# Attention phase of a fused recurrent and feed-forward kernel: one small DMA sent by ACT instead of SP, low parts taken a third of a head later, and turned rows' banks by turns

## The reference, cut to what matters

```python
def _attention(x, Wq, Wk, Wv, Wo):          # 8 batches, 16 heads of 32 features
    q = (x @ Wq.T).reshape(b, s, H, HD)
    k = (x @ Wk.T).reshape(b, s, H, HD)
    v = (x @ Wv.T).reshape(b, s, H, HD)
    scores = jnp.einsum('bqhd,bkhd->bhqk', q, k) / np.sqrt(HD).astype(np.float32)
    scores = jnp.where(causal, scores, jnp.finfo(scores.dtype).min)
    probs = jax.nn.softmax(scores, axis=-1)
    out = jnp.einsum('bhqk,bkhd->bqhd', probs, v).reshape(b, s, d)
    return out @ Wo.T
...
mod = MOD_SCALE * jnp.tanh(attn @ A)
gate_pre = h @ W_in_base.T + mod * (h @ A) @ B
```

## Time and profile before

| | us |
|---|---|
| median of three runs | 2830.97 |
| profiled execution, its own time | 2831.37 |
| its span, first to last instruction | 2829.6 |
| attention in that span | about 870 to 1722 |
| PE busy over the span | 2561.5 |
| DVE busy | 1428.4 |
| ACT busy | 1073.6 |
| POOL busy | 380.9 |

### The profile page before, as it was taken

How to read it: one execution, slowest core, us unless ns; L and a number is a source line. 1 busy time by engine, 2 the same in 40 slices (tenths; PEclk the granted TensorE clock), 3 DMA queues, 4 the chain that set the end, 5 groups by cost and what they waited for, 6 DMA issues and landing times.

```text
span 2829.6 us, 38755 instructions
## 1 busy us (share of the span) xinstructions
PE 2561.5 (91%) x14359; PEld 2059.7 (73%) x14359; DVE 1428.4 (50%) x2943; ACT 1073.6 (38%) x1770; POOL 380.9 (13%) x353
## 2 busy tenths in 40 slices
PE   5899999999995688988898887999999999999997
PEld 4677778777774466766666766888888878888886
DVE  5666656656654356766676775221211423333333
ACT  4444444444442156655665674111111211111111
POOL 0000000000001223332334231000000001111111
PEclk8999999999996888988999987999999999999999
DMA  3000000000002344333433323111111322222212
GB/s 128 15 16 16 30 30 1 30 31 16 1 16 94 110 112 116 80 102 109 117 84 98 98 82 114 45 45 45 45 45 45 123 101 93 109 96 90 90 60 75
DMA packets 97728, 194.60 MB, mean 69 GB/s; under 512 B 22128, under 2 KB 22640, under 8 KB 91376
## 3 DMA queue, kind: packets, MB, share of 16 engines
q1 hardware_dynamic: 97536, 192.04, 21.6%
HBM read 99.43 MB, written 41.94 MB: 50 GB/s over the span
## 4 chain that ended last, share of the span: by engine, by line
PE 78%; DVE 9%; issue 5%; ACT 4%; POOL 2%; DMA 1%; SPq 1%; DVEq 0%; POOLq 0%; ACTq 0%
PE PS L72 13%; PE PS L74 13%; PE PS L73 13%; PE PS L1833 4%; PE PS L1834 4%; PE PS L1835 4%; PE PS L1432 3%; PE PS L695 2%; PE PS L693 2%; PE PS L1451 2%; PE PS L694 2%; PE PS L1408 2%; PE PS L1410 2%; PE PS L1409 2%; DVE PS L1621 1%
## 5 line engine op out<-in xcount | busy, mean ns | idle before, releaser
L1882 DVE TENSOR_TENSOR GF<-SG,PS 128x512 f32<-128x512 f32 x128 | 88.0, 687 | 619.4 <-PE PS L74 619.4
L1621 DVE CUSTOM_DVE_ANT_0 PS<-PS,MK 128x512 f32<-128x512 f32 (+3 forms) x512 | 243.7, 508 | 102.6 <-PE PS L1432 101.5
L1536 ACT ACTIVATE PF<-PS 128x512 f32<-128x512 f32 (+1 forms) x384 | 198.8, 524 | 161.1 <-PE PS L1453 152.6
L1856 ACT ACTIVATE SG<-PS 128x512 f32<-128x512 f32 x128 | 76.3, 596 | 429.6 <-PE PS L1815 429.6
L1451 PE MATMUL PS<-QS,KS 97*128 97x512 f32 (+3 forms) x512 | 184.3, 390 | 56.5 <-issue 42.8
L1432 PE MATMUL PS<-KS,QS 96*128 96x512 f32 (+3 forms) x512 | 183.5, 401 | 38.4 <-DVE MX L1621 38.1
L72 PE MATMUL PS<-XH,WH 128*128 128x512 f32 x512 | 212.1, 414 | 6.5 <-DVE XC L967 6.5
L1860 ACT CAST GH<-GF 128x512 fp32r<-128x512 f32 x128 | 79.3, 620 | 364.1 <-DVE GF L1882 364.1
L1913 POOL TENSOR_SCALAR XN<-XT,MEAN,RSTD 128x512 f32<-128x512 f32 x32 | 67.1, 2101 | 1041.9 <-DMA M<-m_scratch 726.2
L72 PE MATMUL PS<-FH,GW 128*128 128x512 f32 x512 | 200.3, 391 | 7.7 <-DVE DW L1877 7.7
L1833 PE MATMUL PS<-DW,GH 128*128 128x512 f32 x512 | 200.3, 391 | 5.4 <-DVE GL L1884 5.4
(11 more groups left out here) (277 smaller groups left out, 5930.5 us busy)
## 6 DMA issues: line engine op xcount, KB each, us to landing
QS<-QT SPq DMA_DIRECT2D x384, 64.0 KB, 2.0
KS<-QT SPq DMA_DIRECT2D x384, 64.0 KB, 2.0
FH<-rh_scratch SPq DMA_DIRECT2D x16, 1024.0 KB, 5.6
FL<-rl_scratch SPq DMA_DIRECT2D x16, 1024.0 KB, 8.0
XF<-in_x_dram SPq DMA_DIRECT2D x32, 256.0 KB, 3.5
s_scratch<-ZS SPq DMA_DIRECT2D x8, 1024.0 KB, 4.3
STGB<-in_x_dram SPq DMA_DIRECT2D x8, 1024.0 KB, 6.7
rh_scratch<-RH SPq DMA_DIRECT2D x8, 1024.0 KB, 8.7
```

What stands on the lines that cost most here:

```text
L1536: act.activation(PE_[u][:, o:o + at], PS[4 + a % 2][:, 0:at], ACT.Exp, scale=SC).then_inc(a_ex, 1)
L1621: dve.tensor_tensor_reduce(out=p[:, at:at + n], in0=p[:, at:at + n], in1=MK[:, 512 - n:512], scale=1.0, scalar=NEG, op0=ALU.add, op1=ALU.m ...
```

## The change

One table by third of a head takes the place of the generator `attn_order`, and several kinds of steps get a second name, one or a few thirds later, at which the engine that needs another engine's result takes its turn. PE's steps keep their thirds.

- ACT sends the DMA from NM to QS (`largest_out`), one third after it has negated the maxima. SP no longer has a step `largest_in`.
- One third later than before stand on DVE the low parts of turned rows (`normal_low`) and of queries and keys (`project_low`), on ACT, DVE and POOL the splitting of the values (`values_split`), on ACT the copy of the low-rank product (`low_rank_out`), on POOL its piece of the remainder (`remainder_end`). ACT still copies turned rows, queries and keys in the third in which PE computes them.
- DVE's four operations after every fourth head stand at thirds 17, 19, 20 and 21 instead of all at 17; the modulation's at one, two and three thirds after the transposition instead of in the same third.
- The four turned rows of a batch use banks 0, 1, 0, 1 instead of 0, 1, 1, 0.
- The second `largest_in` of a batch and the `modulation` each share a third with a piece of `project`; they now stand ahead of it.

The core of the diff:

```diff
-        for kind, bank, at in (("normal", (0, 1, 1, 0), (46, 47, 0, 1)), ("values", (1, 1, 1, 1), (14, 16, 25, 27)),
-                               ("largest_in", (0, 1, 1, 0), (42, 6, 18, 30)), ("low_rank", (1,), (38,)),
-                               ("modulation", (0,), (10,))):
...
+        for third in range(-72, 3 * HEADS + 24):
+            g, p = divmod(third, 3)
...
+            if p == 0 and 0 <= g - 1 < HEADS:
+                at(third, "remainder", g - 1)
+            if p == 1 and 0 <= g - 1 < HEADS:
+                at(third, "remainder_end", g - 1)
...
+        for b in range(NB):
+            t = 48 * b - 48
...
+            for d, third, bank in ((0, -2, 0), (1, -1, 1), (2, 0, 0), (3, 1, 1)):
+                bank_of["normal", b, d] = bank
+                at(t + third, "normal", b, d)
+                at(t + third + 1, "normal_low", b, d)
+            for r, q, k in ((0, 3, 8), (1, 14, 20), (2, 25, 31), (3, 36, 42)):
+                for n, third in ((0, q), (1, k)):
+                    bank_of["project", 4 * b + r, n] = n
+                    for c in range(4):
+                        at(t + third + c, "project", 4 * b + r, (n, c))
+                    at(t + third + 4, "project_low", 4 * b + r, n)
+            for J, third in enumerate((14, 16, 25, 27)):
+                bank_of["values", b, J] = 1
+                at(t + third, "values", b, J)
+                at(t + third + 1, "values_split", b, J)
...
+            for w, bank in ((4 * b, 0), (4 * b + 1, 1), (4 * b + 2, 1), (4 * b + 3, 0)):
+                bank_of["largest_in", w] = bank
+                at(12 * w - 6, "largest_in", w)
+                at(12 * w - 5, "largest_out", w)
+                at(12 * w + 17, "inverse", w)
+                at(12 * w + 19, "divided", w)
+                at(12 * w + 20, "summed", w)
+                at(12 * w + 21, "gathered", w)
...
-                elif kind == "largest_in":
-                    w, r = a, a % 4
-                    sp.wait_ge(a_ni, w + 1)
-                    if w >= 4:
-                        sp.wait_ge(a_wt, 12 * (w - 4) + 12)
-                    sp.dma_start(f32(QS[96:97, 4 * r:4 * r + 4, :]), f32(NM[w % 2][:, :])).then_inc(a_nm[r], 16)
...
+                elif kind == "largest_out":
+                    r = a % 4
+                    act.wait_ge(a_ni, a + 1)
+                    if a >= 4:
+                        act.wait_ge(a_wt, 12 * (a - 4) + 12)
+                    act.dma_start(f32(QS[96:97, 4 * r:4 * r + 4, :]), f32(NM[a % 2][:, :])).then_inc(a_nm[r], 16)
...
-                elif kind == "project" and how[1] == 3:
-                    n = how[0]
-                    dve.wait_ge(a_qh, 2 * a + n + 1)
...
+                elif kind == "project_low":
+                    dve.wait_ge(a_qh, 2 * a + how + 1)
```

More of the change, by code:

```diff
@@ L1254, in attn_order @@
[L1254 to L1285, removed]
@@ L1287, in build, with at @@
-        steps = [w for g in range(-24, HEADS + 4) for w in attn_order(g)]
+        def at(third, kind, a, how=None):
+            thirds.setdefault(third, []).append((kind, a, how))
+        for third in range(-72, 3 * HEADS + 24):
+            g, p = divmod(third, 3)
+            if 0 <= g < HEADS:
+                at(third, "weights", third, ((0,), (1, 3), (2,))[p])
+            if 0 <= g + 6 < HEADS:
+                at(third, "largest", third + 18, ((3,), (2, 0), (1,))[p])
+            if p == 0 and 0 <= g - 1 < HEADS:
+                at(third, "remainder", g - 1)
+            if p == 1 and 0 <= g - 1 < HEADS:
+                at(third, "remainder_end", g - 1)
+            if p == 0 and 0 <= g - 2 < HEADS:
+                at(third, "mixed", g - 2)
+            if p == 1 and g % 2 and 0 <= g - 3 < HEADS:
+                at(third, "drawn", (g - 3) // 2)
@@ new lines, in build @@
+        for b in range(NB):
+            t = 48 * b - 48
+            for k in range(4):
+                at(t - 22 + 3 * k, "scaled", b, k)
+            for d, third, bank in ((0, -2, 0), (1, -1, 1), (2, 0, 0), (3, 1, 1)):
[12 more added lines that the diff above has]
+                at(t + third + 1, "values_split", b, J)
+            bank_of["low_rank", b] = 1
+            at(t + 38, "low_rank", b)
+            at(t + 39, "low_rank_out", b)
+            for w, bank in ((4 * b, 0), (4 * b + 1, 1), (4 * b + 2, 1), (4 * b + 3, 0)):
[6 more added lines that the diff above has]
+                at(12 * w + 21, "gathered", w)
+            bank_of["modulation", b] = 0
+            at(t + 106, "modulation", b)
+            at(t + 107, "modulated", b)
+            at(t + 108, "modulation_out", b)
+            at(t + 109, "modulation_low", b)
@@ L1289, in build @@
+        steps = [w for third in sorted(thirds) for w in thirds[third]]
         turn01, frees01 = {}, ([], [])
@@ L1511, in attn_scalar @@
                     act.copy(QT[n][a % 2][0][:, :], bank01(kind, a, n)[:, :]).then_inc(a_qh, 1)
-                elif kind == "values":
-                    p3 = bank01(kind, a, how)[:, 0:256].rearrange("p (h r) -> p h r", r=R)
+                elif kind == "values_split":
+                    p3 = bank01("values", a, how)[:, 0:256].rearrange("p (h r) -> p h r", r=R)
                     act.wait_ge(a_vl, 4 * a + how + 1)
@@ L1522, in attn_scalar @@
                         act.wait_ge(a_mo, 2 * (a - 2) + 1)
-                    act.copy(HA[a % 2][:, :], bank01(kind, a)[0:R, :]).then_inc(a_ha, 1)
+                    act.copy(HA[a % 2][:, :], bank01("low_rank", a)[0:R, :]).then_inc(a_ha, 1)
                 elif kind == "largest_in":
@@ L1641, in attn_vector @@
                                       ALU.add).then_inc(a_sm, 1)
-                    if a % 4:
-                        dve.wait_ge(a_sm, sm(a, 3))
-                        dve.tensor_tensor(AM[:, :, :], AM[:, :, :], AM2[:, :, :], ALU.add).then_inc(a_sm, 1)
-                elif kind == "modulation":
-                    c = slice(S * a, S * a + S)
+                elif kind == "gathered" and a % 4:
+                    dve.wait_ge(a_sm, sm(a, 3))
+                    dve.tensor_tensor(AM[:, :, :], AM[:, :, :], AM2[:, :, :], ALU.add).then_inc(a_sm, 1)
+                elif kind == "modulated":
                     dve.wait_ge(a_th, 3 * a + 1)
@@ L1676, in attn_pool @@
                     pool.tensor_tensor(V[:, how, :, 32:48], v3, V[:, how, :, 16:32], ALU.subtract).then_inc(a_vp, 1)
-                elif kind == "remainder":
+                elif kind == "remainder_end":
                     u = a % 2
```

47 lines of the change are left out of this document (22 added, 25 removed).

## The result

The changed kernel took 2753.02 us (median of four runs, 2752.78 to 2753.78) against 2830.72 of the kernel before on the same chips: a ratio of 0.9725 (0.9709 to 0.9742), 78 us less. Forecast were 108 us less, 2723 us; the measured time lies inside the range of 2690 to 2768, but outside the forecast's own 2700 to 2745.

A forecast was written before the change was run, and what follows sets the result against it. PE was taken as the bound, losing time in the attention to waits and the lower clock behind them. Gains 74 + 20 + 14 = 108 us took 2829.6 to 2721.6, forecast 2723 us; range 2690 to 2768, its own 2700 to 2745.

The forecast's parts named there:

- the DMA of the maxima: Attention, PE's waits for the negated maxima sent by SP behind 3 MB: sending from ACT saves 51.9 us of waits.
- The bound taken for the landing: Time for the negated maxima to land without 3 MB ahead: between nothing and 9.1 us, taken near zero.
- ACT's issues at 0: ACT's 32 issues of the negated maxima, about 20 to 28 us of its time: counted 0, at most 28.
- The term of 22 us of clock behind the stall: PE work at the lower clock behind the waits for the negated maxima: 2.2 + 4.2 + 16 = 22 us gained.
- The 74 us: Gain from ACT sending the negated maxima: 51.9 us of waits plus 22 us of clock.
- Banks by turns: Third turned row takes the bank freed earlier: 10 us of waits and 10 us of clock gained, 20 us.
- A third later: DVE's later steps find ACT's copies of values and QT done: 60 us at stake, less 19 and 27, net 14.
- The three new waits named: PE's waits for banks held longer, at three places in seven batches, 1.3 us each: 27 us lost.
- POOL has over half its time free: Reason given for counting the remaining parts of the change, POOL's work among them, at 0.
- The modulation's transposition: The only step waiting for DVE's four operations after every fourth head, one third behind the last: counted 0.
- only the DMA's stall goes: Rival: DVE is the bound and longer held banks take back the shift's gain; gain 74, time 2757 us, chance 0.17.
- The signs: Expected profile: maxima's wait gone, DVE's copy waits near zero, batches 78 to 81 us; over 84 with PE waiting meant wrong.

The follow-up runs named there:

- the fastest kernel: The changed kernel with POOL's four scalings five thirds later and DVE's remainder behind the low parts that share its third: 2708.63 us, ratio 0.9567.
- the kernel with the low parts first: The changed kernel with DVE's remainder behind, not ahead of, the low parts that share its third: 2736.06 us, ratio 0.9671.

## Why the prediction was right and where it was off

It was right on what bounds the kernel and on what its largest gain would be. The sum was 30 us too high, and the measured time lies in the range by its upper end, which had been taken in for a rival.

- **What bounds the kernel, and the DMA of the maxima: right.** The waits on "issue" were this DMA, and the place behind the load and the stores their cause. All 51.9 us of waits went with that part alone. The bound taken for the landing, near zero, held; the first stall of the kernel before had a number for it, 1.3 us. ACT's issues at 0 held as well.
- **The term of 22 us of clock behind the stall: mis-sized.** 13.1 us of PE's time came back, and new waits took it again: the stall had hidden ACT's work on the modulation, and PE's waits for ACT's exponentials rose from 4.2 to 15.0 us. The sum had no term for a wait that a shorter stall uncovers. The 74 us became 52.
- **Banks by turns, 20 us: right in place, shown as 25** against the changed kernel with the old banks, and 0 where the stall still stood behind. The new wait of the fourth row was 0.9 us. The clock's half was read too high: 3.4 us at the lower clock stand behind the wait of the third row in four batches, not in six.
- **A third later, net 14: the step that failed.** With ACT sending and the old banks it brought 0. The waits for the maxima did fall by 33 us (19 were left standing in the sum, 4.9 stood). The three new waits named cost 17.7 us (6.1, 5.9 and 5.7), where 27 were written, but a fourth that was not named, the maxima's transposition behind the values, cost 7.0. "A third later the copy is done when DVE comes" was true of queries and keys and false of the values, since the change moves ACT's copy of them too: DVE still waits 32.2 us for it, and taking the values' splitting back gains 27 us.
- **"POOL has over half its time free": the other step that failed.** That is the share of a batch; in its third quarter POOL had 14.34 us of work in 19.59. With the values handed over a third later, PE waits 25.5 us for POOL instead of 3.4, and in four of the seven batches the clock falls behind it; moving POOL's scalings away gains 22 us. The modulation's transposition, counted at 0 as well, costs 7 us more (10.6 in 8 waits, of which 3.6 stood before).
- **The end.** The last batch and what follows took 79.5 us instead of 77.6; some gain was expected there.
- **Rivals.** The time is within 4 us of that of "only the DMA's stall goes" (2757), which had 0.17, and part of its mechanism is there: what the shift wins is taken back. But it is taken back by POOL (22 us of new waits) as well as by the longer held banks (24.7), and the 78 us are 52 for the stall, 25 for the banks and next to nothing for the later thirds, not 74 and nothing. That the two numbers agree is luck. DVE's load did not set the pace; in the fastest kernel it is busy 63.5 us of 77.9.
- **The signs.** Those on the DMA, the third and fourth turned row, QT and the clock came true. Those on the values' copy and on batches of 78 to 81 us did not, and three batches stand just above the 84 us that would have meant "wrong", though for POOL and not for the banks or the maxima alone.

The account of the batch shown: 94.5 to 83.3 us, where 79.2 were forecast; 3.7 of the 4.1 are the two waits for POOL (2.79 and 0.95). The batches of 84.8 us have the lower clock behind these on top.

## What to carry to other kernels

A small transfer that something waits for should not stand in a queue behind large ones: move it ahead or to another engine's queue. While that queue sets the time, a gain upstream of it hardly shows. Before counting on what stands behind a long stall, ask what the other engines did under its cover: that work comes to light when the stall goes. When a step is moved later for one engine's sake, follow the whole chain that hangs on its result, and read each engine's busy time in the quarter where it has its burst. Check in the diff that the engine that is waited for doesn't move along with the one that waits.

## What the runs showed of the hardware

- A DMA issued from ACT (ACTq, 0.58 to 0.6 us, 1.29 us the first time) ran beside ACT's own exponential. In the table of queues of the changed kernel its traffic is a queue of its own, q10, with 256 packets of the 97536 that q1 had in the kernel before.
- The DMA of 8 KB landed 1.3 us after its issue with small copies ahead of it, and 9.1 us after it behind 3 MB in the same queue.
- The clock at the end of the attention is not tied to what is gained before. In the changed kernel it fell at 1584.4, after gaps of 1.28, 0.43 and 1.13 us in 5 us, and stayed at its lower level for 65 us, into the feed-forward part, though PE was busy 15.50 of 15.96 us in one stretch of it:

```profile
1598.49:1614.45 15.96, 15.50 (x126) 11.85 (x125) 11.44 (x28) 11.73 (x19) 6.11 (x6) 0.50 0.01 3
```

In the kernel with the low parts first it was at its upper level over nearly the same heads, and fell only at 1596.4, for 34 us:

```profile
1581.00:1595.00 14.00, 10.56 (x130) 7.80 (x129) 12.22 (x33) 12.03 (x20) 5.42 (x7) 1.00 0.46 189
```

That is worth up to 7 us between kernels (79.5 and 72.2 from the eighth batch to the feed-forward part). The fastest kernel again had 65 us at the lower level there. Why it did not rise is open.
- POOL's operations take longer where DVE's remainder (L1637) began before them. In the changed kernel, from 960 to 1640, the second operation on the values (L1687) took 1.72 to 1.74 us in the 14 cases beside the remainder and 0.67 in the 16 others, 15 of which lie beside other work of DVE. One of the 14:

```profile
1198.56 1.22 DVE L1637 TENSOR_TENSOR PL<-PF,PH 128x1024 f16<-128x1024 f32 x1
```

```profile
1198.59 1.72 POOL L1687 TENSOR_TENSOR VB<-V,VB 128x256 bf16<-128x256 f32 x1
```

Where POOL's began 0.3 us ahead of DVE's, it took 0.67 us and DVE's remainder 1.42 instead of 1.22. It looks as if the one that comes second waits for the first. No experiment changed this alone.
